# Four-layer pre-norm transformer: the first head pair of each attention layer prepared through four PSUM banks, and 128-column matmuls written as two 64-column halves

## The reference

```python
def _L0_attn_ref(x, W_Q, b_Q, W_K, b_K, W_V, b_V, W_O, b_O):
    Q = jnp.einsum('btd,hkd->bthk', x, W_Q) + b_Q
    K = jnp.einsum('btd,hkd->bthk', x, W_K) + b_K
    V = jnp.einsum('btd,hkd->bthk', x, W_V) + b_V
    scores = jnp.einsum('bqhk,bshk->bhqs', Q, K) / jnp.sqrt(jnp.asarray(d_head, x.dtype))
    attn = jax.nn.softmax(scores, axis=-1)
    out_h = jnp.einsum('bhqs,bshk->bqhk', attn, V)
    return jnp.einsum('bqhk,hdk->bqd', out_h, W_O) + b_O
...
x = x + _L0_attn_ref(_layernorm(x, axis=-1), ...)
x = x + _L0_ffn_ref(_layernorm(x, axis=-1), ...)
x = x + _L1_attn_ref(_layernorm(x, axis=-1), ...)
x = x + _L1_ffn_ref(_layernorm(x, axis=-1), ...)
x = x + _L2_attn_ref(_layernorm(x, axis=-1), ...)
x = x + _L2_ffn_ref(_layernorm(x, axis=-1), ...)
x = x + _L3_attn_ref(_layernorm(x, axis=-1), ...)
x = x + _L3_ffn_ref(_layernorm(x, axis=-1), ...)
```

## Time and profile before

| | us |
|---|---|
| median of three runs | 4273.28 |
| the profiled execution, its own time | 4270.37 |
| its span, first to last instruction | 4268.3 |
| PE busy (23765 matmuls) | 3801.8 (89%) |
| DVE busy | 2967.2 (70%) |
| ACT busy | 2270.2 (53%) |
| share of PE in the chain that ended last | 72% |
| share of DVE, ACT, issue in it | 15%, 6%, 6% |
| line 543 (Q, K projections), 384 instructions | 238.2 |
| line 549 (V), 768 instructions | 122.8 |
| line 566 (output projection), 768 instructions | 115.6 |
| line 926 (exponentials) | 1266.1 |
| line 1110 (running sums) | 1361.4 |

### The profile page before, as it was taken

The page is one execution under the profiler, slowest core; times in us unless marked ns, Lnnn a source line. Parts: engine busy times, 40 slices in busy tenths (PEclk is TensorE's granted clock), DMA queues, the critical chain, the costliest instruction groups (busy, mean ns, idle before and its releaser), DMA issues.

```text
span 4268.3 us, 65152 instructions
## 1 busy us (share of the span) xinstructions
PE 3801.8 (89%) x23765; PEld 1843.1 (43%) x23765; DVE 2967.2 (70%) x5821; ACT 2270.2 (53%) x2635; POOL 10.9 (0%) x16
## 2 busy tenths in 40 slices
PE   3899999999999867898988996759999999999997
PEld 2344444444444333444444443324444444444444
DVE  3677877777777664666656666337877877777774
ACT  1566666666666413555545553326666665666663
POOL 1000000000000000000000000000000000000000
PEclk9999999999999977999999998859999999999998
DMA  1000000000000000000000000000000000000000
GB/s 49 6 8 9 9 9 9 11 7 11 6 9 9 13 0 6 11 14 11 14 10 14 10 11 8 13 7 7 9 9 9 11 7 12 8 9 7 9 6 18
DMA packets 44413, 44.38 MB, mean 10 GB/s; under 512 B 16466, under 2 KB 30554, under 8 KB 43834
## 3 DMA queue, kind: packets, MB, share of 16 engines
q1 hardware_dynamic: 44090, 40.09, 3.2%
HBM read 37.56 MB, written 1.70 MB: 9 GB/s over the span
## 4 chain that ended last, share of the span: by engine, by line
PE 72%; DVE 15%; issue 6%; ACT 6%; SPq 1%; DMA 1%; ACTq 0%; DVEq 0%
PE ps L523 58%; PE ps L543 5%; DVE over L1129 4%; DVE acc L1110 3%; ACT work L926 3%; PE ps L549 3%; PE ps L566 3%; ACT over L936 1%; DVE x L1253 1%; PE ps L804 1%; PE ps L793 1%; PE ps L512 1%; DVE stats L1026 1%; DVE oN L1088 1%; DVE Kl L1053 1%
## 5 line engine op out<-in xcount | busy, mean ns | idle before, releaser
L926 ACT ACTIVATE work<-ps 128x1024 f32<-128x1024 f32 (+1 forms) x1344 | 1266.1, 992 | 1239.2 <-PE ps L523 1239.2
L1110 DVE TENSOR_TENSOR acc<-acc,work 128x1024 f32<-128x1024 f32 (+2 forms) x1152 | 1361.4, 1182 | 330.7 <-ACT work L926 269.0
L523 PE MATMUL ps<-work,V 128*64 128x512 f32 (+3 forms) x5376 | 1260.2, 590 | 0.0
L936 ACT ACTIVATE over<-ps 128x1024 f32<-128x1024 f32 (+1 forms) x672 | 672.5, 1001 | 115.6 <-PE ps L523 115.2
L1129 DVE CUSTOM_DVE_ANT_0 over<-ps,over,mpart 128x512 f32<-128x512 f32 (+1 forms) x752 | 490.7, 689 | 242.9 <-PE ps L523 239.5
L523 PE MATMUL ps<-Qh,Kh 64*128 64x512 f32 (+3 forms) x2688 | 649.0, 479 | 8.3 <-issue 4.6
L523 PEld LDWEIGHTS ps<-work,V 128*64 128x64 f32 x5376 | 334.9, 136 | 596.4 <-issue 460.9
L1129 DVE CUSTOM_DVE_ANT_0 over<-ps,over 128x512 f32<-128x512 f32 (+3 forms) x752 | 423.0, 601 | 207.1 <-PE ps L523 204.8
L523 PE MATMUL ps<-Qh,Kl 64*128 64x512 f32 (+3 forms) x2688 | 526.4, 387 | 0.0
L523 PE MATMUL ps<-Ql,Kh 64*128 64x512 f32 (+3 forms) x2688 | 521.7, 384 | 0.0
L523 PE MATMUL ps<-auxQ,auxK 64*128 64x512 bf16 (+3 forms) x2688 | 519.0, 381 | 0.0
(11 more groups left out here) (181 smaller groups left out, 2238.9 us busy)
## 6 DMA issues: line engine op xcount, KB each, us to landing
rden<-inverse_sums SPq DMA_DIRECT2D x192, 128.0 KB, 2.9
auxQ<-mrow SPq DMA_DIRECT2D x384, 1.0 KB
wqk<-in_wqk SPq DMA_DIRECT2D x24, 128.0 KB, 2.4
dcomp<-den SPq DMA_DIRECT2D x192, 2.0 KB
wv<-in_wv SPq DMA_DIRECT2D x24, 64.0 KB, 2.2
inverse_sums<-rcomp SPq DMA_DIRECT2D x96, 4.0 KB, 1.3
work<-in_mlp_w SPq DMA_DIRECT2D x1, 1024.0 KB
work<-in_c_aux SPq DMA_DIRECT2D x1, 1024.0 KB, 4.8
```

The lines of the kernel that those rows point to most:

```text
L523: return pe.matmul(o, w, m, start=start, stop=stop, skip_group_check=True)
L926: act.activation(work[:, 2 * e:2 * e + 2, q0:CH], ps[:, 2 * two:2 * two + 2, q0:CH], ACT.Exp, scale=L.scale).then_inc(s["p_ready"], 1)
L936: act.activation(over[:, :, 0:w], ps[:, MAXB:MAXB + 2, 0:w], ACT.Relu).then_inc(s["relu_ready"], 1)
L1110: dve.tensor_tensor(o, o, work[:, slots[two]:slots[two] + 2, q0:CH], ALU.add).then_inc(s["acc_ready"], 1)
```

## The change

The stage with preparation alone is replaced by `opening`, written for each engine from one list, `Layer.opening`. Jobs go through banks 0 to 3 in turn, units through banks 4, 5 and 6, 7 in turn (the second pair clips into the last two slots of `work`). PE waits before `excess` of unit u only for the maxima of unit u-2, and puts a unit's `base` behind the next item of the list. PE starts each projection once its chunk of `yT` is there. Independently of this, every Q, K, V and output projection, in all stages, is written as two matmuls of 64 output partitions, and the `mt` transpose as a plain matmul against the identity with 64 columns. The third layer's bias rows and the first output weights are loaded ahead of the second pair's weights.

```diff
+        early = [u for u in range(self.U) if self.unit_at[u] < 0]
+        mts = [c for c, k in enumerate(mt_at) if k < 0]
+        self.opening, units = [], list(early)
+        ahead = 2 if causal else 5
+        others = self.qk[ahead:] + [("V", c) for c in range(NC)]
+        for kind, c in self.qk[:ahead]:
+            self.opening.append(("job", kind, c))
+        if featured:
+            self.opening.append(("unit", units.pop(0)))
+        while units or others or mts:
+            while mts and (not units or units[0] >= self.chunk_units(mts[0])):
+                self.opening.append(("job", "mt", mts.pop(0)))
+            ready = not others or all(self.qk_needed(g[1]) <= 8 - sum(o[0] != "V" for o in others)
+                                      for u in units[:1] for g in self.units[u])
+            if units and ready:
+                self.opening.append(("unit", units.pop(0)))
+            if others:
+                self.opening.append(("job", *others.pop(0)))
...
+    def opening_items(self):
+        jobs, units = 0, 0
+        for item in self.opening:
+            if item[0] == "job":
+                yield (*item, jobs % 4)
+                jobs += 1
+            else:
+                yield (*item, None, MAXB + 2 * (units % 2))
+                units += 1
...
-        mcol = sb("mcol", [P, NC, 2 * TPC])
+        mcol = sb("mcol", [P, NC, DH])
...
+        def excess_of(b):
+            return over if b == MAXB else work[:, 2 * RING - 2:2 * RING, :]
...
-                        cols = slice(0, P) if kind == "Q" else slice(P, 2 * P)
-                        pe.matmul(bank(MISC), wqk[p][:, cols], yv[:, c * CH:(c + 1) * CH],
-                                  start=True, stop=True).then_inc(s["proj_ready"], 1)
+                        w = 0 if kind == "Q" else P
+                        for h2 in range(2):
+                            ins = mm(ps[head(h2), b, :], wqk[p][:, w + h2 * DH:w + (h2 + 1) * DH],
+                                     yv[:, c * CH:(c + 1) * CH], True, True)
+                        ins.then_inc(s["proj_ready"], 1)
...
                         for t in range(TPC):
-                            ins = pe.matmul(ps[:, MISC, t * P:(t + 1) * P],
-                                            yv[:, (c * TPC + t) * P:(c * TPC + t + 1) * P], wv[p][:],
-                                            start=True, stop=True)
+                            for h2 in range(2):
+                                k0 = (c * TPC + t) * P + h2 * DH
+                                ins = mm(ps[head(h2), b, t * P:(t + 1) * P], yv[:, k0:k0 + DH], wv[p][:], True, True)
...
-                        pe.transpose(ps[0:2 * TPC, MISC, 0:P], mcol[:, c, :], ident[:]).then_inc(s["mt_psum"], 1)
+                        mm(ps[0:DH, b, 0:P], mcol[:, c, :], ident[:], True, True).then_inc(s["mt_psum"], 1)
...
                         for t in range(TPC):
-                            ins = pe.matmul(ps[:, MISC, t * P:(t + 1) * P], oN[:, t * P:(t + 1) * P], wo[p][:],
-                                            start=True, stop=True)
+                            for h2 in range(2):
+                                k0 = t * P + h2 * DH
+                                ins = mm(ps[head(h2), MISC, t * P:(t + 1) * P], oN[:, k0:k0 + DH], wo[p][:], True, True)
...
-                def excess(h, p, u):
-                    at_least(pe, s["top_ready"], L.NTOP * h + L.tops_to[u])
+                def excess(h, p, u, b0=MAXB, back=0):
+                    at_least(pe, s["top_ready"], L.NTOP * h + L.tops_to[max(u - back, 0)])
...
+                def opening():
+                    based = None
+                    for what, kind, c, b in L.opening_items():
+                        if kind == "mt" and based is not None:
+                            base(0, 0, *based)
+                            based = None
+                        if what == "job":
+                            if kind != "mt":
+                                pe.wait_ge(yt_ready, NC * LN_OF[L.n] + max(c, b) + 1)
+                            if job_at[b] is not None:
+                                released(*job_at[b])
+                            job(kind, 0, c, 0, b)
+                            job_at[b] = (kind, 0, c)
+                        elif L.units[kind][0][0] == "tile0":
+                            pe.wait_ge(s["bias_in"], 64)
+                            tile0(0, 0, b)
+                        else:
+                            excess(0, 0, kind, b, 1)
+                        if based is not None:
+                            base(0, 0, *based)
+                        based = (kind, b) if what == "unit" and L.units[kind][0][0] != "tile0" else None
+                    if based is not None:
+                        base(0, 0, *based)
+                    pe.wait_ge(s["v_ready"], NC)
...
+                def opening():
+                    for what, kind, c, b in L.opening_items():
+                        if what == "job":
+                            job(kind, 0, c, 0, b)
+                        else:
+                            tops(0, kind, b)
```

More of the change, by code:

```diff
@@ L53, in head, with each_stage @@
     return slice(h2 * DH, (h2 + 1) * DH)
-def each_stage(fori, stage):
-    stage(-1, 1, (False, False, False), main=False, prep=True, tail=False)
+def each_stage(fori, opening, stage):
+    opening()
     stage(0, 0, (False, True, False), main=True, prep=True, tail=False)
@@ L154, in __init__ @@
         self.jobs += [(k, 0, "op", c) for c, k in enumerate(op_at)]
+        early = [u for u in range(self.U) if self.unit_at[u] < 0]
[16 more added lines that the diff above has]
+                self.opening.append(("job", *others.pop(0)))
+        self.n_open = len(early)
         self.later = [(k + 1, 1, "inv", c) for c, k in enumerate(den_at)]
@@ L478, in stage @@
                                 inverse_in(n + rel, c)
-                load_pair(0, 0)
-                sp.wait_ge(s["wqk_in"], 16 * L.loads)
-                sp.wait_ge(s["wv_in"], 16)
-                load_pair(1, 1)
-                each_stage(None, stage)
+                def opening():
+                    load_pair(0, 0)
+                    load_out(0, 0)
+                    if L.featured:
+                        load_bias(0, 0)
+                    sp.wait_ge(s["wqk_in"], 16 * L.loads)
+                    sp.wait_ge(s["wv_in"], 16)
+                    load_pair(1, 1)
+                    for what, kind, c, b in L.opening_items():
+                        if what == "job" and kind == "mt":
+                            max_rows(0, c, 0)
+                each_stage(None, opening, stage)
                 sums_out(PAIRS - 1, NC - 1)
@@ L536, in released, with job @@
                         pe.wait_ge(s["x_added"], NC * h + c + 1)
-                def job(kind, h, c, p):
+                def job(kind, h, c, p, b=MISC):
                     if kind in ("Q", "K"):
@@ L587, in scores, with tile0 @@
                     ins.then_inc(s["st_ready"], 1)
-                def tile0(h, p):
+                def tile0(h, p, b0=MAXB):
                     pe.wait_ge(s["hi_ready"], 8 * h + L.qk_needed(0))
@@ L705, in stage @@
                                 base(n + rel, par[rel], u)
-                each_stage(pe.Fori, stage)
+                def opening():
[22 more added lines that the diff above has]
+                    pe.wait_ge(s["v_ready"], NC)
+                job_at = [None] * 4
+                each_stage(pe.Fori, opening, stage)
                 last = PAIRS - 1
@@ L902, in job @@
                         dst, w = (Qh, 0) if kind == "Q" else (Kh, 1)
-                        act.activation(dst[p][:, c * CH:(c + 1) * CH], bank(MISC), ACT.Identity,
+                        act.activation(dst[p][:, c * CH:(c + 1) * CH], bank(b), ACT.Identity,
                                        bias=bqk[:, p, w:w + 1]).then_inc(s["hi_ready"], 1)
@@ L906, in job @@
                         act.wait_ge(s["v_psum"], NC * h + c + 1)
-                        act.activation(V[p][:, c * TPC:(c + 1) * TPC, :].rearrange("p t d -> p (t d)"), bank(MISC),
+                        act.activation(V[p][:, c * TPC:(c + 1) * TPC, :].rearrange("p t d -> p (t d)"), bank(b),
                                        ACT.Copy).then_inc(s["v_ready"], 1)
@@ L941, in stage, with opening @@
                             copy_out(n + rel, c)
-                each_stage(act.Fori, stage)
+                def opening():
+                    for what, kind, c, b in L.opening_items():
+                        if what == "job":
+                            job(kind, 0, c, 0, b)
+                        elif L.units[kind][0][0] != "tile0":
+                            w = L.units[kind][-1][2] + L.units[kind][-1][4] * P
+                            act.wait_ge(s["md_ready"], L.relus_to[kind] + 1)
+                            act.activation(excess_of(b)[:, :, 0:w], ps[:, b:b + 2, 0:w], ACT.Relu).then_inc(s["relu_ready"], 1)
```

(3 more changed lines are left out.)

46 lines of the change are left out of this document (22 added, 24 removed).

## The result

The changed kernel takes 4068.45 us, 4273.28 before: a ratio of 0.9503, with a 95% interval of 0.9488 to 0.9518. This is the middle one of three runs: 4058.89 us (the profiled one), 4068.45, and a slow one of 9509.04, which the ratio leaves out. With two runs 9.6 us apart, a difference of a few us from 4068 says nothing. Forecast were 4094, with a range of 4057 to 4150.

A forecast was written before the change was run, and what follows sets the result against it. PE's order of work bounds the steady part; in the openings no engine is full and each waits for the other. 4270.4 - 148 (openings) - 31 (halves) = 4091, 4094 for the median; range 4057 to 4150.

The forecast's parts named there:

- Front of an opening: First layer's opening, until the fourth `Kd` is ready: 9 us, taken between 7.5 and 10.2.
- Rounds with a job: First layer's opening: seven units, each with a job, three at DVE's 2.2 us and four at 2.0, 14.6 us.
- Tail: End of the first layer's opening: `mt` waits for all maxima of the first eight units, scores at about 9.5 us.
- granted clock near 1.00 in the openings: Sign for the forecast: PE at the high clock in the new openings, where 0.52 and 0.50 were granted before.
- Totals: Whole openings of the three layers: 33.1, 36 and 35 us instead of 84.7, 79.9 and 87.8.
- The price of the low clock: Rival, 20%: the clock stays low through the new openings, some 12 us a layer, 37 in all, 4131 us.
- The halves, per job: Steady stages: a projection takes 0.91 us instead of 1.06, a V or output job 0.96 instead of 1.09.
- loads not covered: Rival, 4%: in V and output jobs each small half waits for its load, 1.94 us a job, 4262 us.
- a bound by instructions: Rival, 3%: short V and output jobs are bound by instruction count, 2.18 us a job, slower at 4305 us.
- The discount: Only 63% of the halves' 48 us reach the end, 31 us, as PE then waits longer for DVE.
- Maxima's matmul at nothing: The `mt` matmul goes from one to two instructions and loses a change of shape: no gain booked.
- First scores at the low clock: First scores after the openings ran at the low clock before: up to 3 us a layer more, left to the range.

The follow-up runs named there:

- e5_qk: The kernel before with only the Q and K projections in halves: 4259.79 us, ratio 0.9962.
- e6_vop: The kernel before with only V and the output projection in halves: 4243.24 us, ratio 0.9926.
- e11_mt: The kernel before with only the maxima's matmul in the new form (64 columns, two instructions): 4275.20 us, ratio 1.0005.

## Why the prediction was right, and where not

The sign, the two separate gains and their order of size held: forecast -148 and -31, measured -157 in the openings of the profile (-150 by the run of the openings alone) and -51. The mechanism of the openings was the one described, and three of its terms were off in ways that partly cancel.

- **Front of an opening** (9 us taken). It is 6.4 (52.25 to 58.60). The prediction put it between PE's low-clock pace and DVE's; the five projections came at 0.95 us each, at the high level from the first (in the third layer, where PE had stood idle for 12.08 us, at 1.49). DVE's four K's set its length: 7.5 us was the bound given for that, and it came out shorter still, since a first projection at the high level takes 1.1 and not 2.05.
- **Rounds with a job** (14.6 for seven). 13.3 (58.60 to 71.88). All run at 1.84 to 1.95; a round with a Q, for which I had taken DVE's 2.2, is not longer. PE waits only for the maxima of two units back, which I had not used.
- **Tail** (9.5). 10.6. Its waits were as described, longest the stop of 1.7 us at the maxima; the low clock behind it was not foreseen here, and the sign "granted clock near 1.00 in the openings" held in one of three.
- **Totals** 33.1, 36 and 35 against 30.2, 31.5 and 33.6. The second depends on the clock: in other kernels with the same list it was 35 to 37, which is what was forecast, so some 5 us of the profile's lead there are luck.
- **The price of the low clock** (37 us over three layers). One unit buffer and one bank showed its kind: 26 us more of PE's busy time in each. In the change itself the step between the levels gave 59 of the 157 us. The prediction's walk has this in its durations at the high clock without giving it as a sum.
- **The halves, per job.** 0.91 for a projection and 0.92 to 0.93 for V and output, forecast 0.91 and 0.96. The number of jobs was wrong: 348 were counted, 288 stand ahead of values. By their distances they give 20 + 25 = 45 us, and 25 + 23 = 48 were booked; the larger gain of the small jobs hid the smaller number. Of the 51 measured, 6 stay unexplained. The two rivals on them, loads not covered and a bound by instructions, are out: neither 1.94 nor 2.18 us a job. The rule on loads and row groups of the Trainium skill ("TensorE: Matmul & The Clock Gate", The mechanism) did not hold for column halves here, at 128 columns either: 16 loads and 16 matmuls of an output take 0.93 us together.
- **The discount** (63% of 48). This is the term that failed: all 51 us arrived. I had let every early arrival at a wait for DVE be lost. PE's waits for the maxima were 27.9 us in 30 before and 28.5 in 31 after in the first layer's main part. They did not grow, nor did they in `e5_qk` and `e6_vop` (28.0 in 30 in both). I read this so: DVE's and ACT's work hangs on PE's, and what PE gains elsewhere in the pair moves the late maxima forward as well; no run tried it by itself. In the causal layer the discount had a grain of truth: the 20 projections ahead of an output save nothing, since the output waits for their remainder (32.1 us before, 32.5 in `e5_qk`).
- **Maxima's matmul at nothing.** Right, 1.0005.
- **First scores at the low clock**, left to the range. They still run at 0.63 in the first and third layer (82.46 and 2674.57), so nothing came of it there; in the second they run at 0.40.

Of the 26 us between 4094 and 4068, the table gives 9 to the openings and 20 to the halves; the starts and stretches between the layers add 3. Of these 32 us 7 are the profiled run's luck: it lies 10 below the median where 3 were allowed for.

## What to carry to other kernels

A stretch in which no engine is full is worth more than its waits when PE's clock is low there: look at the durations of its matmuls. A fix that thins out PE's rounds can lose the level again and bring new waits, as it did here. Where small matmuls stand between matmuls of another tile shape, write them in their neighbours' shape: it is free, and a change cost 0.15 us here. Count only the jobs that have such a neighbour. A wait is not a fixed tax: before discounting a gain by it, ask whether the late engine's own input comes from the one that got faster, and read which two jobs share its step; changing such tables was worth 37 and about 50 us here.

## What the runs showed of the hardware

Matmuls of two jobs in the same shape of 128 rows by 64 columns can run beside each other. PE's timeline at a maxima's job in the new form, which writes partitions 0 to 63 only, and the values behind it:

```profile
238.01 0.32 PE L565 MATMUL ps<-ident,mcol 128*64 128x128 f32 x1
238.02 0.64 PE L565 MATMUL ps<-work,V 128*64 128x512 f32 x1
238.17 0.27 PE L565 MATMUL ps<-ident,mcol 128*64 128x128 f32 x1
238.28 1.88 PE L565 MATMUL ps<-work,V 128*64 128x512 f32 x7
```

The first values' matmul starts 0.01 us after the first `mt` instruction, ahead of the second. That it is one of the other column half is a reading; the rows don't give the half. From `mt` to the rest of the values it is 0.27 us, 0.21 from `mt` to the values before, and the time with one instruction more 92 times was the same (`e11_mt`, 1.0005).

The clock's level was not a function of a stretch's own instructions alone: one opening ran at 1.00 in one kernel and at 0.80 to 0.85 in others with the same list. PE's busy share doesn't order the levels either, since slow matmuls fill the time themselves: a stretch with PE busy 9.38 of 10 us was at 1.00, one with 7.67 of 10 at 0.50, and the first 10 us of the changed kernel's second opening, with 6.31 busy, at 1.00.

The granted clock can be shown wrong at the start of a trace. In the first opening before the change it reads 1.00 (53 to 137, PE busy 41.78 us), in `e11_mt`, with the same opening of 84.7 us, 0.50:

```profile
53.00:137.00 84.00, 42.11 (x92) 17.47 (x92) 23.07 (x56) 18.82 (x24) 0.00 (x0) 0.50 0.00 0
```

A projection takes 2.04 us there, as in the third opening, which reads 0.50. Durations are the safer reading.
